# A vision layer's expert stage: the first layer in one stretch, the turned marks copied by two engines, two output tiles

## What is computed

```python
xf = x.reshape(-1, D)                      # 16384 tokens, D = 64
logits = xf @ router_w.T + router_b        # 32 experts
idx = jnp.argmax(logits, axis=-1)
h = jnp.einsum('nd,ndh->nh', xf, jnp.take(W1, idx, axis=0)) + jnp.take(b1, idx, axis=0)
h = jax.nn.relu(h)                         # 16 hidden values
out = jnp.einsum('nh,nhd->nd', h, jnp.take(W2, idx, axis=0)) + jnp.take(b2, idx, axis=0)
out = jax.nn.relu(out)
```

## Time and profile before

| | us |
|---|---|
| median of 3 runs | 618.31 (617.52 to 618.47) |
| the profiled execution | 618.27 |
| its span in the trace | 616.5 |
| mean granted TensorE clock | 0.96 of full speed |
| last stage in the trace | from 395.8 to the end |

### The profile page before, as it was taken

One profiled execution on the slowest core, in us unless ns is written; L12 is line 12 of the kernel. 1 busy time (PEld: TensorE's weight loads), 2 busy tenths in 40 slices (PEclk: granted clock), 3 DMA queues, 4 the chain that ended last, 5 costly groups with the idle time before them and its releaser, 6 DMA issues. The chain is left out here.

```text
span 616.5 us, 18701 instructions
## 1 busy us (share of the span) xinstructions
PE 552.0 (90%) x7273; PEld 394.3 (64%) x7274; DVE 490.0 (79%) x879; ACT 408.8 (66%) x723; POOL 350.1 (57%) x388
## 2 busy tenths in 40 slices
PE   5897999999999999999656776499999999999995
PEld 4796789999898899897212222355555555555552
DVE  4798788888888888886799999677777777777762
ACT  2475788888888888888697576135555555555543
POOL 8303367778779887774898698542333423334220
PEclk9999899999999999999779788879999999999998
DMA  9622222222222222210000000001011010110101
GB/s 193 107 41 46 59 62 57 59 59 57 63 59 54 59 58 61 62 35 3 1 0 0 0 1 2 3 3 26 18 24 22 21 25 19 23 22 21 26 19 27
DMA packets 62381, 23.05 MB, mean 37 GB/s; under 512 B 45780, under 2 KB 62292, under 8 KB 62292
## 3 DMA queue, kind: packets, MB, share of 16 engines
q1 hardware_dynamic: 61472, 21.69, 17.2%
q10 hardware_dynamic: 692, 0.13, 0.1%
q0 software_dynamic: 128, 0.00, 0.0%
HBM read 5.02 MB, written 4.19 MB: 15 GB/s over the span
## 5 line engine op out<-in xcount | busy, mean ns | idle before, releaser
L762 DVE TENSOR_REDUCE work<-psum 128x16 f32<-128x1024 f32 x64 | 78.0, 1218 | 31.2 <-PE psum L597 31.2
L697 ACT ACTIVATE work<-work 128x1024 f32<-128x1024 f32 x64 | 67.8, 1060 | 23.5 <-DVE work L767 23.2
L1788 ACT ACTIVATE hid<-psum,b1c 128x512 f32<-128x512 f32 x96 | 58.9, 684 | 32.2 <-PE psum L1695 32.2
L767 DVE TENSOR_TENSOR work<-psum,work 128x1024 f32<-128x1024 f32 x64 | 78.3, 1224 | 2.2
L1678 POOL TENSOR_TENSOR m_sq<-m_xc 128x256 f32<-128x256 f32 x32 | 19.6, 613 | 100.1 <-DVE m_xc L1839 100.0
L705 ACT ACTIVATE work<-psum 128x512 f32<-128x512 f32 x128 | 70.7, 618 | 2.4 <-PE psum L612 1.5
L612 PE MATMUL psum<-kc,work 128*128 128x128 f32 x512 | 67.7, 275 | 4.2 <-ACT work L697 3.5
L1703 PE MATMUL psum<-x_t,w1x 64*64 64x256 f32 x1024 | 70.9, 393 | 0.0
L628 PEld LDWEIGHTS psum<-work 128*64 128x64 f32 x2048 | 62.3, 138 | 5.3 <-issue 5.3
L628 PE MATMUL psum<-work 128*64 128x18 f32 x2048 | 65.5, 212 | 0.0
L612 PEld LDWEIGHTS psum<-kc,work 128*128 128x128 f32 x512 | 58.8, 141 | 8.7 <-ACT work L697 4.4
(11 more groups left out here) (197 smaller groups left out, 1291.4 us busy)
## 6 DMA issues: line engine op xcount, KB each, us to landing
work<-big_bc SPq DMA_DIRECT2D x256, 32.0 KB, 2.0
h_all<-in_x SPq DMA_DIRECT2D x16, 256.0 KB, 5.3
work<-big_a SPq DMA_DIRECT2D x32, 128.0 KB, 2.2
out<-out_st SPq DMA_DIRECT2D x128, 32.0 KB
w1x<-in_L_ffn_W SPq DMA_DIRECT2D x2, 128.0 KB, 4.1
kc<-constants SPq DMA_DIRECT2D x1, 202.0 KB, 2.7
w2x<-in_L_ffn_W SPq DMA_DIRECT2D x1, 128.0 KB, 4.1
work<-in_L_tok_qkv_w ACTq DMA_DIRECT2D x2, 32.0 KB, 2.5
```

Source lines behind the costliest of these rows:

```text
L697: act.activation(prob[:, f], prob[:, f], ACT.Exp).then_inc(prob_done, 1)
L762: dve.tensor_reduce(top[:, f, :].rearrange("p (g h) -> p g h", g=4), sc, AX.X, ALU.max).then_inc(top_done, 1)
L767: dve.tensor_tensor(prob[:, f].rearrange("p (g h) k -> p g h k", g=4), sc, top[:, f, :].rearrange("p (g h) -> p g h", g=4).unsqueeze(3).br ...
L1788: act.activation(hid[:, g, :], psum[:, HID_BANK[g], :], ACT.Relu, bias=b1c[:, g:g + 1]).then_inc(relu_act, 1)
```

## The change

What it does:
- PE: all eight first-layer parts stand in one stretch at the head of a pass, with waits on `x_half` ahead of parts 5 and 7. The marks go to two banks (b = 0 to bank 2, columns 0 to 255; b = 1 to bank 6, columns 256 to 511) and signal after each two matmuls. Masks follow the xh turn directly. The y turn, now of group i + 1, stands between masks and logits.
- The turned marks are copied by ACT (256 columns, `mark_act`) and DVE (256 columns, `mark_dve`).
- ACT stages y after the relus. DVE's pass begins with its copy; the h, nsum, xc of group i + 1 stand between relu and router, ssum and var at the end.
- `out_st` has two tiles with a semaphore each; SP's loop is written out, and the last group's four stores are issued by SP and ACT, two each.

The diff, cut to its core:

```diff
-def store_quad(eng, out, src, i, done):
+def store_quad(eng, out, src, i, done, parts=(0, 1, 2, 3)):
...
+    for n in parts:
+        k, b2 = n // 2, n % 2
+        a = flat[bass.ds(at + (k * 16 + b2 * L), 1), :]
...
+        eng.dma_start(dst, src[:, 2 * k + b2, :]).then_inc(done, 16)
...
-    out_st = sb("out_st", [P, 4, C])
+    out_st = sb("out_st", [P, 2, 4, C])
...
-    mark_turned, mark_copied = sem("mark_turned"), sem("mark_copied")
+    mark_turned, mark_act, mark_dve = sem("mark_turned"), sem("mark_act"), sem("mark_dve")
...
-    out_made, stored = sem("out_made"), sem("stored")
+    out_made, stored = sem("out_made"), (sem("stored0"), sem("stored1"))
...
-        for i in range(LAST + 1):
+        for i in range(-2, LAST + 1):
...
-            with sp.Fori(0, QUADS) as i:
+            for i in range(QUADS):
                 sp.wait_ge(out_made, i + 1)
-                store_quad(sp, out, out_st[:, :, :], i, stored)
-            sp.wait_ge(stored, QUADS * 64)
+                store_quad(sp, out, out_st[:, i % 2], i, stored[i % 2], (0, 1) if i == QUADS - 1 else (0, 1, 2, 3))
+            for par in range(2):
+                sp.wait_ge(stored[par], QUADS // 2 * 64)
...
-                if live(i, 0):
-                    pe.wait_ge(y_staged, i + 1)
-                    if not first(i):
-                        pe.wait_ge(h_done, i)
-                    if not first(i, 3):
-                        pe.wait_ge(out_made, i - 3)
-                    for n in range(2):
-                        m = pe.transpose(psum[:, 0, n * P:n * P + P], y_st[:, n, :], ident)
-                    m.then_inc(y_turned, 1)
                 if live(i, 2):
                     pe.wait_ge(x_copied, i - 1)
-                    for g, b in X_PARTS[:4]:
-                        x_part(i - 2, g, b, True)
+                    for n, (g, b) in enumerate(X_PARTS):
+                        if n in (4, 6):
+
+                            pe.wait_ge(x_half, i * 16 - 32 + (n - 2) * 2)
+                        x_part(i - 2, g, b, n < 4)
...
                     pe.wait_ge(chosen, i - 1)
                     if not first(i, 2):
-                        pe.wait_ge(mark_copied, i - 2)
-                    for s in range(4):
-                        if s == 3:
-
-                            pe.wait_ge(x_half, i * 16 - 24)
-                        m = pe.matmul(psum[0:96, 2, s % 2 * 256 + s // 2 * P:s % 2 * 256 + s // 2 * P + P],
-                                      mark[:, s, :, :].rearrange("p j e -> p (j e)"), ident_b[:, :],
-                                      start=True, stop=True, skip_group_check=True)
-                    m.then_inc(mark_turned, 1)
+                        pe.wait_ge(mark_act, i - 2)
+                        pe.wait_ge(mark_dve, i - 2)
+                        pe.wait_ge(o_copied, i - 2)
+                    for b in range(2):
+                        for k in range(2):
+                            m = pe.matmul(psum[0:96, (2, 6)[b], 256 * b + k * P:256 * b + k * P + P],
+                                          mark[:, 2 * k + b, :, :].rearrange("p j e -> p (j e)"), ident_b[:, :],
+                                          start=True, stop=True, skip_group_check=True)
+                        m.then_inc(mark_turned, 1)
                 if live(i, 3):
-                    pe.wait_ge(o_copied, i - 2)
+                    if i == LAST:
+                        pe.wait_ge(o_copied, i - 2)
                     pe.wait_ge(h_done, min(i + 1, QUADS))
...
                 if live(i, 2):
-                    for g, b in X_PARTS[4:]:
-                        x_part(i - 2, g, b, False)
                     if first(i, 2):
                         pe.wait_ge(masks_set, 2)
-                    pe.wait_ge(mark_copied, i - 1)
+                    pe.wait_ge(mark_act, i - 1)
+                    pe.wait_ge(mark_dve, i - 1)
                     for g in range(4):
                         mask(g)
+                if live(i, -1):
+                    pe.wait_ge(y_staged, i + 2)
+                    if not first(i, -1):
+                        pe.wait_ge(h_done, i + 1)
+                    if live(i, 3):
+                        pe.wait_ge(out_made, i - 2)
+                    for n in range(2):
+                        m = pe.transpose(psum[:, 0, n * P:n * P + P], y_st[:, n, :], ident)
+                    m.then_inc(y_turned, 1)
...
                 if live(i, 2):
-                    if not first(i, 2):
-                        pe.wait_ge(o_copied, i - 2)
...
-            stage_y(0)
-
             def body(i):
-                if live(i, -1):
-                    act.wait_ge(y_turned, i + 1)
-                    stage_y(i + 1)
                 if live(i, 2):
-                    act.wait_ge(mark_turned, i - 1)
-                    act.activation(mark_t[:, :, :].rearrange("p b q -> p (b q)"), psum[0:96, 2, :], ACT.Copy
-                                   ).then_inc(mark_copied, 1)
+                    act.wait_ge(mark_turned, i * 2 - 3)
+                    act.activation(mark_t[:, 0, :], psum[0:96, 2, 0:256], ACT.Copy).then_inc(mark_act, 1)
...
+                if live(i, -2):
+                    if i >= -1:
+                        act.wait_ge(y_turned, i + 2)
+                    stage_y(i + 2)
+                if live(i, 2):
                     act.wait_ge(o_done, i * 2 - 2)
...
+            act.wait_ge(out_made, QUADS)
+            store_quad(act, out, out_st[:, (QUADS - 1) % 2], QUADS - 1, stored[(QUADS - 1) % 2], (2, 3))
...
-                if live(i, 0):
-                    h = h_all[:, bass.ds(i * 4, 4), :]
-                    dve.wait_ge(y_turned, i + 1)
-                    dve.tensor_tensor(h, h, psum[:, 0, 0:256].rearrange("p (s d) -> p s d", s=4), ALU.add
-                                      ).then_inc(h_done, 1)
...
-                    dve.wait_ge(nsum_done, i + 1)
-
-                    if not first(i):
-                        dve.wait_ge(xh_done, i)
-                    dve.scalar_tensor_tensor(xc[:, :, :], nsum[:, :].unsqueeze(2).broadcast_to([P, 4, C]),
-                                             1.0 / C, h, ALU.mult, ALU.add).then_inc(xc_done, 1)
+                if live(i, 2):
+                    dve.wait_ge(mark_turned, i * 2 - 2)
+                    dve.tensor_copy(mark_t[:, 1, :], psum[0:96, 6, 256:512]).then_inc(mark_dve, 1)
                 if live(i, 3):
                     dve.wait_ge(o_turned, i - 2)
 
-                    if not first(i, 3):
-                        dve.wait_ge(stored, i * 64 - 192)
-                    dve.scalar_tensor_tensor(out_st[:, :, :], psum[:, 0, 256:512].rearrange("p (s d) -> p s d", s=4),
+                    if not first(i, 4):
+                        dve.wait_ge(stored[(i - 3) % 2], (i - 3) // 2 * 64)
+                    dve.scalar_tensor_tensor(out_st[:, (i - 3) % 2], psum[:, 0, 256:512].rearrange("p (s d) -> p s d", s=4),
                                              0.0, h_all[:, bass.ds(i * 4 - 12, 4), :], ALU.max, ALU.add
                                              ).then_inc(out_made, 1)
...
+                if live(i, -1):
+                    h = h_all[:, bass.ds(i * 4 + 4, 4), :]
+                    dve.wait_ge(y_turned, i + 2)
+                    dve.tensor_tensor(h, h, psum[:, 0, 0:256].rearrange("p (s d) -> p s d", s=4), ALU.add
...
+                    dve.wait_ge(nsum_done, i + 2)
+
+                    if not first(i, -1):
+                        dve.wait_ge(xh_done, i + 1)
+                    dve.scalar_tensor_tensor(xc[:, :, :], nsum[:, :].unsqueeze(2).broadcast_to([P, 4, C]),
+                                             1.0 / C, h, ALU.mult, ALU.add).then_inc(xc_done, 1)
                 if live(i, 1):
 
                     dve.wait_ge(logits_done, i)
...
-                        dve.wait_ge(mark_turned, i - 1)
+                        dve.wait_ge(mark_turned, i * 2 - 2)
...
                                       ).then_inc(chosen, 1)
+                if live(i, -1):
+                    dve.wait_ge(sq_done, i + 2)
+                    dve.tensor_reduce(ssum[:, :], sq[:, :, :], AX.X, ALU.add).then_inc(ssum_done, 1)
+                    dve.wait_ge(ssum_done, i + 2)
+                    dve.tensor_scalar(var[:, :], ssum[:, :], 1.0 / C, LN_EPS, ALU.mult, ALU.add
+                                      ).then_inc(var_done, 1)
```

21 lines of the change are left out of this document (6 added, 15 removed).

## The result

The changed kernel takes **609.57 us** (median of 4 runs, 608.46 to 610.79), the kernel before 617.91 (617.29 to 618.47) beside it: a ratio of **0.9866, 95% interval 0.9839 to 0.9893**, so 1.3% faster. The predicted 612.3 was on the right side and 2.7 us too high; 609.57 lies just inside the lower end of the forecast's own band, 609.5 to 614. The profiled execution took 610.79, its span is 609.0.

What follows compares the result with a forecast made beforehand. PE's seamless row was taken as the bound, period 6.26 us against 6.41. Terms -4.2 + 0.2 + 0.65 - 0.4 - 2.2 = -5.95 on 618.27 gave 612.3; forecast band 609.5 to 614 (chance 0.60), range 607 to 616.

Steps and rivals of the forecast that it cites:

- Step 1: On PE, both first-layer halves in one stretch: 1.88 us, a gain of 0.17 per group, with x_half waits costing 0.
- Step 2: On PE, the y turn moved ahead of the logits: 0.28 plus 0.54 us, a gain of 0.14 per group.
- Step 3: On PE, the four mark matmuls lose their middle wait: o turn 0.31 us after the first mark, a gain of 0.03.
- Step 4: Ahead of PE's masks, an exposed wait for DVE's mark copy: masks 1.05 us after the first mark, PE idle 0.19 per group.
- Steps 5 and 6: PE's other waits stay covered (room 0.2 to 0.3 us); DVE has room 0.4 before the mark, 0.25 before the copy.
- The start: At the stage's start, DVE's longer row delays the marks, and the next first layer comes at 412.4 instead of 411.73: +0.65 us.
- The end: At the kernel's end, last output tile -0.4 us with two tiles; last stores -2.2 us, shared by SP and ACT.
- A: Rival at PE's masks: cover isn't needed, masks start 0.86 us after the first mark; -5.9, total 606.4; chance 0.12.
- C: Rival on DVE's row: its loop becomes the bound at 6.55 us per group; +9.0, total 621.3; chance 0.05.
- B: Rival on PE's row: x_half waits exposed or masks at 1.2; +0.1 to +0.2 us per group, 615.4 to 618.5; chance 0.13.
- D: Rival at start or end: clock late or stores in turn; +1.4 to +3.1 us, 613.7 to 615.4; chance 0.10.

## Why the prediction was right or wrong

**The reading of the bound** was right. PE's row sets the period: no more work on DVE matters up to half a microsecond, and every change of PE's blocks shows in full.

**Step 1, the joined first layer**: 1.89 measured, 1.88 predicted, the x_half waits cost nothing. Right. What the step didn't say is that joining also carries the new DVE order (the loop above); it was worth more than its own 0.17.

**Step 2, y turn and logits**: 0.27 + 0.49 against 0.28 + 0.54. This is the largest mis-sized term: -0.20 per group instead of -0.14. The step took 0.05 off the logits, the front of a foreign block, where the rows now show 0.10. That the borders' price is one of tile shape is read from the places of the blocks; no kernel changed a block's shape alone.

**Step 3, the marks**: 0.26 instead of 0.31. The fourth mark was taken as 0.21 behind the first, and the block's end as 0.10. The fourth does start 0.21 behind the first, but the o turn follows 0.06 behind the fourth, as close as one mark behind another: the marks and the o turn don't pay a border between them that the sum had charged.

**Step 4, the wait in the cover's place**: 1.05 predicted, 1.03 measured, 0.16 idle instead of 0.19, DVE's copy 0.42 as taken. The place is right, by two errors that nearly cancel: the copy starts 0.05 earlier (0.46 after the first mark, not 0.51), and the wake takes 0.15, not 0.12. The price of the wait is not: without it the masks would stand at 0.80, not 0.86, so it costs some 0.23 by starts where the step had 0.19. The step also read the wake by the number of semaphores, 0.05 on one and 0.14 on two. With the waits swapped it is 0.05 on two: what counts is which of them is late. The Trainium skill, VectorE: DVE Perf Modes, section "The TRN2 errata", would give an estimated 0.39 for the copy. Every row of it here is 0.41 to 0.42, so the measured row was the better price.

**Steps 5 and 6, waits that stay covered and DVE's room**: right. No wait but the masks' is in PE's list, DVE's room ahead of the mark is 0.56 instead of 0.4 and ahead of the copy 0.49 instead of 0.25, its busy time 5.1 instead of 5.4, since steps that don't wait for each other overlap.

The period's error of 0.11 is thus 0.05 of logits, 0.02 to 0.03 of `b2p` and the second layer (1.95 to 1.96 instead of 1.98 to the next first layer), 0.02 of the masks' place and 0.01 each of the masks' block and the y turn: small terms, nearly all on one side, times 28 is the 3.1 us.

**The start**: +0.25 instead of +0.65. The marks come at 409.07, 11.49 after the first y turn, where the sum had 11.65; the masks 1.00 later instead of 1.15; the next first layer 3.24 after those instead of 3.33. The term's shape held (DVE's longer row, behind a stretch of 32 first-layer records that takes 3.69 at half clock), and three small excesses made it 0.4 too large. One of them is a slip of the sum: 405.07 + 0.42 + 5 x 0.33 + 0.56 is 407.7, not 407.8.

```profile
404.88 3.69 PE L1704 MATMUL psum<-x_t,w1x 64*64 64x256 f32 x32
...
409.07 0.40 PE L1727 MATMUL psum<-ident_b,mark 128*96 128x128 bf16 x4 [0.49 <-DVE mark L1882]
...
410.07 0.59 PE L1696 MATMUL psum<-mark_t,off 32*128 32x512 bf16 x4 [0.38 <-DVE mark_t L1832]
```

**The end**: -0.43 for the tile, as summed. The stores were too optimistic by 0.7: the term "half of 3.14" assumed that ACT issues like SP. The Trainium skill, DMA: Bandwidth & Descriptors, section "Issuing engines are not separate DMA queues", says that issuing from several engines saves only issue time. The rows agree that nothing but issue time was saved (1.75 from the last issue's end to the span's end, shared or not), but show that it isn't saved in full: 2.12 for ACT's two, where SP takes 1.25.

**The rivals.** A (masks at 0.86) and C (DVE's loop the bound) didn't come about in the kernel as changed. C's mechanism is real and was produced by splitting the first layer again. B's exposed waits didn't appear. D, a short end, did in part: 0.7 of its 1.4.

## What to carry to other kernels

Where an engine's row is seamless, price a block by its borders on both sides and on its neighbours too: here a foreign tile shape costs 0.05 to 0.1 us at either side, and moving two transposes by two places was worth 0.35 per group. Before undoing or copying one part of a reordering, follow the loop through both engines: which steps lie between one block's result and its next request; work that is moved into that loop on one engine has to be paid by work moved out of it on the other. Of two waits ahead of one matmul, put the one that comes late first, and the one that is already met last; it gave 0.08 per group for a swapped line.

## What the runs showed of the hardware that was not expected

- The order of two waits: 0.15 from DVE's end to the matmul's start with DVE's wait second, 0.05 with it first. The one written second is an instruction of its own in the trace, the one written first goes with the weight load.
- ACT's first store issue took 1.44 beside SP's 0.63, with one or two issues on ACT; SP was not slowed.
- DVE starts an instruction that waits for nobody before the one ahead has ended: 0.07 after `var`'s start, which itself is shown as 0.17 long, and 0.33 from one 256-column sum to the next, each shown as 0.41.
- Identical stages took 1.3 us more in the kernel after than before, with a mean granted clock of 0.94 instead of 0.96. A gain of 0.2% in one stage is better read from that stage than from the total.
